# Layer 0's query projection as three products of split float32 values

## Chip, cores and metric

One core of one Trainium2 chip. The metric is the device time of one execution in microseconds (us); the kernel before has a median of 1353.7 us in 3 runs (1352.72 to 1354.24).

## What is computed

Two layers on x of shape (8, 512, 256), each a cross attention (16 heads of 16) and a feed-forward part. The change touches only layer 0's query projection:

```python
qp = (q @ Wq_w.T + Wq_b)          # q = layernorm(x), per batch (512, 256) @ (256, 256)
kp = (k @ Wk_w.T + Wk_b)          # k = ctx
vp = (v @ Wv_w.T + Wv_b)          # v = ctx
scores = einsum('bqhd,bkhd->bhqk', qp, kp) / sqrt(16)
```

The result `qp` is cut into three bfloat16 parts whose sum is the float32 value; attention multiplies those parts.

## The kernel before

`project_phase` is the first of three phases and takes the first 168 us. It runs over 8 batches, written out by hand, and in each makes, from the transposed context `CT`, layer 0's keys (k0), layer 0's values (v0), layer 1's keys (k1) and layer 1's values (v1), and from the normalised and transposed x, layer 0's queries (q0). It stores keys, queries and values to HBM, from where `attention_phase` loads them. Between phases all engines meet at the end of the block.

**TensorE** (L258 to L356), in each batch and in this order: k0 (`columns`, L291), two halves of v0 (`values`, L305), k1, the first half of v1, the transposes of normalised x into two PSUM banks (L338 to L342), the second half of v1 (L343), a count of masked keys (L345), and q0 (L350). `columns` makes two output tiles of 128x512 (m = 0, 1), each as a sum of two float32 products (c = 0, 1). In the profile each float32 matmul stands as two records, so q0's four matmuls are eight records. Seven PSUM banks go round; `room` waits until a bank's last reader is done.

**The copy of x** between the transposes and q0: ScalarE copies chunk 0 from PSUM to `XT` (L421) and VectorE copies chunk 1 (L565), each once per batch, in parallel. TensorE waits for both (L348, L349). `XT` has two buffers.

**ScalarE** (L407 to L425), per batch: `take` k0 (rest and first bfloat16 part, four copies), the square root of the normalisation, the second part of the last batch's q0, the second part of k0 (L401), `take` k1 (L394, four copies), the copy of x, the second part of k1, `take` q0 (L392). In batch 7 it issues nine DMAs of the next phase (`first_group`, L418) ahead of `take` k1.

**VectorE** (L547 to L578), per batch: v0 out of PSUM (L505), `normalize` (L492, L497), the third part of the last q0 (L523), the first half of v1 out, the copy of x (L565), the second half of v1 out, the next mask (L466), the next moments (L483), q0's remainder (`rest_of`, L516), the mask's sums. After batch 7 it runs a short tail (L580 to L592) whose L588 releases TensorE's L352, the last product before the phase ends.

**GpSimd** (L437 to L456) makes a few constants, then runs `split` for k0 and k1 of each batch: L433 subtracts the first part from the rest, L435 the second. ScalarE's second part (L401) waits for L433.

**SyncE** issues the loads and stores in program order. The query weight `wq0` is the 12th load (L217); its semaphore is `q_landed`.

Of the kernel before, what the change touches and what calls it, by code (L numbers as in the profile page):

```python
# [8 lines left out]
F32 = mybir.dt.float32  # L9
# [62 lines left out]
def project_phase(nc, dram, scratch, w, const):  # L72
# [3 lines left out]
    with ExitStack() as mem:  # L76
# [3 lines left out]
        def two(name, shape, dt):  # L80
            return [sb(f"{name}{i}", shape, dt) for i in range(2)]
# [10 lines left out]
        Z_sum = two("a_masked_sum", [P, T], BF16)  # L92
        X = two("a_x", [P, TT, D], F32)
        XN = two("a_xn", [P, TT, D], F32)
        XT = two("a_xT", [P, DC, T], F32)
        stats = two("a_stats", [P, TT, 6], F32)
        mv = two("a_mv", [P, TT, 2], F32)
        rstd = two("a_rstd", [P, TT], F32)
# [159 lines left out]
        @block.tensor  # L258
        def _(pe):
            def column_room(b, n, m):  # L260
                if n in by_pool:
                    pe.wait_ge(rounded[n], taken(n, b, m))
                else:
                    pe.wait_ge(remains[n], rest_made(n, b, m))

            def room(b, p):

                b, p = (b, p - 7) if p >= 7 else (b - 1, p + 5)
                if b < 0:
                    return  # L270
                if p in (0, 1):
                    column_room(b, "k0", p)
                elif p in (2, 3):
                    pe.wait_ge(v_out[0], 2 * b + p - 1)
                elif p in (4, 5):
                    column_room(b, "k1", p - 4)
                elif p in (6, 9):
                    pe.wait_ge(v_out[1], 2 * b + (1 if p == 6 else 2))
                elif p == 7:
                    pe.wait_ge(x_by_act, b + 1)  # L280
                elif p == 8:
                    pe.wait_ge(x_by_dve, b + 1)
                else:
                    column_room(b, "q0", p - 10)

            def out(b, p):
                return bank[(12 * b + p) % 7]

            first = {"k0": 0, "k1": 4, "q0": 10}

            def columns(b, n, src):  # L291

                for m in range(DC):
                    room(b, first[n] + m)
                    o = out(b, first[n] + m)
                    for c in range(DC):
                        mm = pe.matmul(o[:, :], w["w" + n][:, c, m * P:(m + 1) * P], src[:, c, :], start=(c == 0), stop=(c == DC - 1))  # L297
                    mm.then_inc(made[n], 1)

            def count(b):  # L300
                pe.wait_ge(mask_made, mask_summed(b))
                pe.matmul(count_bank[0:NB, :], pick[:, NB - 1 - b:2 * NB - 1 - b], Z_sum[b % 2][:, :], start=(b == 0),
                          stop=(b == NB - 1), skip_group_check=True).then_inc(counted, 1)

            def values(b, l, u):  # L305

                p = (2 + u) if l == 0 else (6, 9)[u]
                room(b, p)
                o = out(b, p)
                for j in range(2):  # L310
                    t = 2 * u + j
                    for c in range(DC):
                        mm = pe.matmul(o[:, j * D:(j + 1) * D], CT[b % 2][:, c, t * P:(t + 1) * P], w[f"wv{l}"][:, c, :], start=(c == 0), stop=(c == DC - 1))  # L313
                mm.then_inc(v_made[l], 1)

            pe.wait_ge(built, 7)
            for _ in range(8):
                pe.matmul(out(0, 11)[:, :], const["less"][:, 0:P], const["less"][:, :], start=True, stop=True)
            for b in range(NB):
                half = b % 2  # L320
                pe.wait_ge(ctx_landed[half], 16 * (b // 2 + 1))
                if b == 0:
                    pe.wait_ge(k0_landed, 32)
                columns(b, "k0", CT[half])
                if b == 0:
                    pe.wait_ge(v0_landed, 16)
                values(b, 0, 0)
                values(b, 0, 1)
                if b == 0:
                    pe.wait_ge(k1_landed, 16)  # L330
                columns(b, "k1", CT[half])
                if b == 0:
                    pe.wait_ge(one_landed, 48)
                values(b, 1, 0)
                if b == 0:
                    pe.wait_ge(cut, 3)
                pe.wait_ge(ln_out, (TT + 1) * (b + 1))
                for c in range(DC):  # L338
                    room(b, 7 + c)
                    for t in range(TT):  # L340
                        mm = pe.transpose(out(b, 7 + c)[:, t * P:(t + 1) * P], XN[half][:, t, c * P:(c + 1) * P], const["ident_f"][:, :])
                    mm.then_inc(x_turned, 1)  # L342
                values(b, 1, 1)  # L343
                for a in ([], [0, 1])[b] if b < 2 else [b]:
                    count(a)  # L345
                if b == 0:
                    pe.wait_ge(q_landed, 32)
                pe.wait_ge(x_by_act, b + 1)  # L348
                pe.wait_ge(x_by_dve, b + 1)  # L349
                columns(b, "q0", XT[half])  # L350
            pe.wait_ge(tail, 6)
            pe.matmul(count_bank[0:1, 0:1], left_top[:, :], const["ones"][0:NB, 0:1], start=True, stop=True).then_inc(counted, 1)  # L352
            keep_busy(pe, const, out(NB - 1, 7), 8)
            pe.wait_ge(tail, 7)
            const["flag"] = pe.value_load(const["general"][0:1, 0:1])
            keep_busy(pe, const, out(NB - 1, 7), 8)  # L356
# [5 lines left out]
        def _(act):  # L362
# [44 lines left out]
            for b in range(NB):  # L407
                half = b % 2
                if b == 0:
                    act.wait_ge(k0_landed, 32)  # L410
                take(b, "k0")
                act.wait_ge(ln_moments, 2 * TT * (b + 1))
                nc.scalar.activation(rstd[half][:, :], mv[half][:, :, 1], ACT.Sqrt, bias=const["eps"][:, 0:1], scale=16.0).then_inc(ln_std, 1)
                if b > 0:
                    next_part(b - 1, "q0")
                next_part(b, "k0")
                if b == NB - 1:
                    first_group()  # L418
                take(b, "k1")
                act.wait_ge(x_turned, 2 * b + 1)  # L420
                nc.scalar.activation(XT[half][:, 0, :], bank[(12 * b + 7) % 7][:, :], ACT.Copy).then_inc(x_by_act, 1)  # L421
                next_part(b, "k1")
                take(b, "q0")
            next_part(NB - 1, "q0")
# [3 lines left out]
        def _(pool):  # L428
# [21 lines left out]
            pool.wait_ge(cut, 8)  # L450
            nc.gpsimd.tensor_copy(qk0[:, :], qk[:, :]).then_inc(cut, 1)
            pool.wait_ge(cut, 9)
            nc.gpsimd.memset(qk0[0:1, 0:1], 0.0)
            for b in range(NB):
                split(b, "k0")
                split(b, "k1")  # L456
# [2 lines left out]
        def _(dve):  # L459
# [87 lines left out]
            for b in range(NB):  # L547
                if b == 0:
                    dve.wait_ge(bv0_landed, 32)
                values(b, 0, 0)  # L550
                values(b, 0, 1)
                normalize(b)
                if b == 0:
                    dve.wait_ge(q_landed, 32)
                    nc.vector.tensor_scalar(w["bq0"][:, :], w["bq0"][:, :], 0.25, None, ALU.mult).then_inc(small_made, 1)
                    dve.wait_ge(small_made, 1)
                    dve.wait_ge(one_landed, 48)
                if b > 0:
                    third_of(b - 1, "q0")
                if b == 1:  # L560
                    mask_of(1)
                    sum_mask(1)
                values(b, 1, 0)
                dve.wait_ge(x_turned, 2 * b + 2)
                nc.vector.tensor_copy(XT[b % 2][:, 1, :], bank[(12 * b + 8) % 7][:, :]).then_inc(x_by_dve, 1)  # L565
                values(b, 1, 1)
                if b == 0:
                    moments(1)
                    rest_of(0, "q0")
                    mask_of(0)  # L570
                    sum_mask(0)
                elif b + 1 < NB:
                    mask_of(b + 1)
                    moments(b + 1)
                    rest_of(b, "q0")
                    sum_mask(b + 1)
                if b == 1:
                    later_weights()  # L578
# [1427 lines left out]
def build(nc, dram):  # L2006

    with ExitStack() as ctx:
# [45 lines left out]
        with ExitStack() as first:  # L2054
            def wsb(name, shape, dt):
                return first.enter_context(nc.sbuf_tensor(name, shape, dt))

            early = {n: wsb(n, [P, DC, D], F32) for n in ("wk0", "wv0", "wq0", "wk1", "wv1")}
            early |= {n: wsb(n, [P, DC], F32) for n in ("bk0", "bq0")}
            early |= {n: wsb(n, [P, 2, D], F32) for n in ("bv0", "bv1")}  # L2060
            project_phase(nc, dram, scratch, w | early, const)
# [44 lines left out]
```

## Time and profile before

| | us |
|---|---|
| median of 3 runs | 1353.7 |
| lowest, highest | 1352.72, 1354.24 |
| the profiled execution's own time | 1358.95 |
| its span | 1357.2 |
| projection phase | 0 to 168 |
| TensorE busy in the span | 1259.6 (93%) |
| VectorE, ScalarE, GpSimd busy | 1003.9 (74%), 867.4 (64%), 511.7 (38%) |

The busy time of TensorE counts overlapping records once; a float32 128x512 record lasts 0.59 us while the next one starts 0.43 us after it, so the distance between starts is the price of a matmul and not its duration. The granted clock is 1.0 for 2.4 GHz and 0.5 for 1.2 GHz.

### The profile page before, as it was taken

The numbers are of one execution on the slowest core, as the hardware profiler recorded it, in microseconds if no ns is written. First come the engines' busy times: TensorE is split into PE (matmuls) and PEld (weight loads), VectorE is DVE, ScalarE is ACT, GpSimd is POOL, SyncE is SP. The second block draws the span as 40 slices with busy tenths as digits, with TensorE's granted clock in tenths as the row PEclk, the third lists the DMA queues.
The fourth block names the chain that finished last, engine by engine and source line by source line (L and its number), as shares of the span: only waits on it lengthen the run. The fifth ranks groups of instructions, "written<-read, shape, count | busy, mean of one in ns | idle before, by whom it ended". The sixth has DMA issues, their size and how long they took to land. (4 is left out here: it accounts for less than half of the span.)

```text
span 1357.2 us, 21436 instructions
## 1 busy us (share of the span) xinstructions
PE 1259.6 (93%) x7571; PEld 652.3 (48%) x7571; DVE 1003.9 (74%) x1724; ACT 867.4 (64%) x1483; POOL 511.7 (38%) x674
## 2 busy tenths in 40 slices
PE   8999989999999999999999999999998999980499
PEld 4565522334343343434455445545553785430298
DVE  5776788797878788786666688888773564996764
ACT  4455427676767777677665655665554666868693
POOL 3555400144353444435565433333333101656600
PEclk9999969999999999999999999999999999995699
DMA  7999774323334242333424553343201001326233
GB/s 242 379 328 329 284 180 115 104 64 93 96 113 127 63 136 79 111 99 100 118 78 115 153 173 95 104 120 98 63 18 48 1 0 47 140 93 232 78 109 109
DMA packets 88074, 170.82 MB, mean 126 GB/s; under 512 B 14742, under 2 KB 49310, under 8 KB 86430
## 3 DMA queue, kind: packets, MB, share of 16 engines
q1 hardware_dynamic: 87083, 167.37, 39.4%
q10 hardware_dynamic: 883, 2.05, 0.7%
q8 instruction: 63, 1.03, 0.3%
q14 instruction: 45, 0.37, 0.1%
HBM read 108.26 MB, written 60.31 MB: 124 GB/s over the span
## 5 line engine op out<-in xcount | busy, mean ns | idle before, releaser
L1342 DVE TENSOR_REDUCE b_neg_max<-b_score 128x1 f32<-128x512 f32 (+3 forms) x864 | 540.8, 662 | 177.8 <-PE b_score L887 93.6
L1112 ACT ACTIVATE b_probs<-b_exp 128x512 f32<-128x512 f32 (+1 forms) x864 | 463.2, 581 | 281.6 <-PE b_exp L911 280.7
L884 PE MATMUL b_score<-b_k_stack,b_q_stack 97*128 97x512 bf16 (+3 forms) x1024 | 355.9, 351 | 10.8 <-issue 4.9
L911 PE MATMUL b_exp<-b_q_stack,b_k_stack 100*128 100x512 bf16 (+3 forms) x1024 | 344.3, 341 | 6.4 <-ACT b_probs L1112 5.6
L932 PE MATMUL b_av<-b_probs,b_values 128*17 128x512 f32 (+3 forms) x2048 | 228.6, 518 | 3.7 <-POOL b_probs L1210 3.5
L884 PEld LDWEIGHTS b_score<-b_k_stack,b_q_stack 97*128 97x128 bf16 x1024 | 99.8, 98 | 246.8 <-DVE b_neg_max L1342 128.5
L911 PEld LDWEIGHTS b_exp<-b_q_stack,b_k_stack 100*128 100x128 bf16 x1024 | 100.1, 98 | 82.5 <-ACT b_probs L1112 24.8
L1210 POOL TENSOR_SCALAR_AFFINE_SELECT b_probs<-b_probs 128x512 f32<-128x512 f32 x96 | 61.7, 643 | 176.8 <-ACT b_probs L1112 176.3
L1218 POOL CAST b_max_parts<-b_neg_max 128x16 bf16<-128x16 f32 x64 | 12.9, 202 | 280.5 <-DVE b_neg_max L1342 278.2
L887 PE MATMUL b_score<-diag_qk,minus_big 128*128 128x128 bf16 x512 | 112.6, 220 | 0.0
L1626 PE MATMUL f_bank<-normed,f_w_upT 128*128 128x512 f32 x192 | 82.7, 592 | 0.0
L1810 POOL TENSOR_TENSOR f_hidden<-f_tmp,f_hidden 128x2048 int32<-128x2048 int32 x8 | 44.2, 5530 | 89.7 <-DVE f_tmp L1760 89.7
L932 PEld LDWEIGHTS b_av<-b_probs,b_values 128*17 128x17 f32 x2048 | 34.1, 95 | 76.5 <-issue 37.0
L968 PE MATMUL b_work<-wo,b_attendedT 128*128 128x256 f32 x256 | 61.5, 383 | 0.3 <-DVE b_x L1283 0.2
L433 POOL TENSOR_TENSOR a_rest_k<-a_rest_k,a_part_k 128x1024 f32<-128x1024 f32 x16 | 38.8, 2427 | 60.8 <-ACT a_part_k L392 49.4
L313 PE MATMUL a_bank<-wv,a_ctxT 128*128 128x256 f32 x256 | 60.5, 385 | 0.0
L887 PEld LDWEIGHTS b_score<-diag_qk,minus_big 128*128 128x128 bf16 x512 | 50.3, 98 | 20.4 <-issue 2.0
L297 PE MATMUL a_bank<-a_ctxT,wk 128*128 128x512 f32 x128 | 57.6, 593 | 0.8 <-DMA bk<-L_bk_in 0.8
L1626 PEld LDWEIGHTS f_bank<-normed,f_w_upT 128*128 128x128 f32 x192 | 36.4, 190 | 45.1 <-issue 43.0
L313 PEld LDWEIGHTS a_bank<-wv,a_ctxT 128*128 128x128 f32 x256 | 48.8, 193 | 13.3 <-issue 7.7
L61 PE MATMUL f_over<-less,ident_b 128*128 128x512 bf16 x31 | 9.7, 477 | 45.8 <-DVE f_hidden L1863 45.1
L968 PEld LDWEIGHTS b_work<-wo,b_attendedT 128*128 128x128 f32 x256 | 47.1, 189 | 9.8 <-DVE b_x L1283 2.1
(231 smaller groups left out, 2026.2 us busy)
## 6 DMA issues: line engine op xcount, KB each, us to landing
b_q_stack<-s_q SPq DMA_DIRECT2D x378, 64.0 KB
s_k<-a_part_k SPq DMA_DIRECT2D x48, 256.0 KB, 3.2
b_k_stack<-s_k SPq DMA_DIRECT2D x60, 192.0 KB
s_up<-f_up SPq DMA_DIRECT2D x6, 1536.0 KB, 5.1
s_va<-a_va SPq DMA_DIRECT2D x16, 544.0 KB, 5.4
b_values<-s_va SPq DMA_DIRECT2D x16, 544.0 KB, 4.2
a_mask_q<-mask_in SPq DMA_DIRECT2D x8, 1024.0 KB, 8.0
b_k_stack<-s_k SPq DMA_DIRECT2D x60, 128.0 KB
```

Source lines behind the costliest of these rows:

```text
L297: mm = pe.matmul(o[:, :], w["w" + n][:, c, m * P:(m + 1) * P], src[:, c, :], start=(c == 0), stop=(c == DC - 1))
L313: mm = pe.matmul(o[:, j * D:(j + 1) * D], CT[b % 2][:, c, t * P:(t + 1) * P], w[f"wv{l}"][:, c, :], start=(c == 0), stop=(c == DC - 1))
L884: mm = pe.matmul(o, q, KS[half][0:R_MAX, h, 0:w], start=True, stop=causal or not general)
L887: mm = pe.matmul(o[:, w - P:w], const["minus_big"][:, :], d[:, :], start=False, stop=True, skip_group_check=True)
L911: mm = pe.matmul(o, k, QS[half][0:NSTACK, h, q0:T], start=True, stop=not masked)
L932: mm = pe.matmul(av_bank[32 * j:32 * j + VW, q0:T], VA[n % 2][:, kc, 4 * g + j, :], probs[kc][:, j, q0:T], start=(kc == 0), stop=(kc == TT ...
L968: mm = pe.matmul(work[:, x * D:(x + 1) * D], src[:, c, y * P:(y + 1) * P], wt[:, c, :], start=(c == 0), stop=(c == DC - 1))
L1112: nc.scalar.activation(probs[kc][:, h0:h0 + m, q0:T], exp_bank[n % RINGS][:, 0:m * w].rearrange("p (h n) -> p h n", h=m), ACT.Exp).then_in ...
L1210: nc.gpsimd.affine_select(out=block, in_=block, fill=0.0, compare_op=ALU.is_ge, base=-1, pattern=[[0, 4], [1, P]], channel_multiplier=-1). ...
L1342: nc.vector.tensor_reduce(neg_max[u][:, qt, h0:h0 + m], score_bank[n % RINGS][:, 0:m * w].rearrange("p (h n) -> p h n", h=m), AX.X, ALU.ma ...
L1626: mm = pe.matmul(bank[f][:, :], w_upT[:, c, f * P:(f + 1) * P], xT[:, b, c, :], start=(c == 0), stop=(c == DC - 1))
L1810: nc.gpsimd.tensor_tensor(whole(b)[:, MINE:FC, :], sig[b % 2][:, MINE:FC, :], whole(b)[:, MINE:FC, :], ALU.mult).then_inc(act_by_pool, 1)
```

## The change

The float32 type "float32r" is a float32 word that TensorE multiplies at reduced precision. The change splits both operands of q0 into a float32r high value and the float32r remainder and sums three products of them: low weight times high x, high weight times high x, high weight times low x, for both c, so six matmuls per output tile and twelve per batch in place of four. The weights are split once on GpSimd, ahead of its first `split`; `query_low` lies on the bytes of `wq0`. x is split from PSUM in each batch: ScalarE copies both chunks to `XT_high`, VectorE subtracts both to `XT_low`, each chunk after ScalarE's copy of it. `XT_high` and `XT_low` have one buffer each. The other projections stay float32.

```diff
-        XT = two("a_xT", [P, DC, T], F32)
+        XT_high, XT_low = sb("a_xT_high", [P, DC, T], F32R), sb("a_xT_low", [P, DC, T], F32R)
+        query_high = sb("a_wq0_high", [P, DC, D], F32R)
+        query_low = nc.alloc_sbuf_tensor_at("a_wq0_low", [P, DC, D], F32R, offset=const["wq0_at"])
...
-                elif p == 7:
-                    pe.wait_ge(x_by_act, b + 1)
-                elif p == 8:
-                    pe.wait_ge(x_by_dve, b + 1)
+                elif p in (7, 8):
+                    pe.wait_ge(x_by_dve, DC * b + p - 6)
...
+            def queries(b):
+
+                for m in range(DC):
+                    room(b, first["q0"] + m)
+                    o = out(b, first["q0"] + m)
+                    terms = [(wt, src, c) for wt, src in ((query_low, XT_high), (query_high, XT_high), (query_high, XT_low)) for c in range(DC)]
+                    for k, (wt, src, c) in enumerate(terms):
+                        mm = pe.matmul(o[:, :], wt[:, c, m * P:(m + 1) * P], src[:, c, :], start=(k == 0), stop=(k == len(terms) - 1))
+                    mm.then_inc(made["q0"], 1)
...
                 if b == 0:
-                    pe.wait_ge(q_landed, 32)
-                pe.wait_ge(x_by_act, b + 1)
-                pe.wait_ge(x_by_dve, b + 1)
-                columns(b, "q0", XT[half])
+                    pe.wait_ge(cut, 12)
+                pe.wait_ge(x_by_dve, DC * (b + 1))
+                queries(b)
...
-                act.wait_ge(x_turned, 2 * b + 1)
-                nc.scalar.activation(XT[half][:, 0, :], bank[(12 * b + 7) % 7][:, :], ACT.Copy).then_inc(x_by_act, 1)
+                for c in range(DC):
+                    act.wait_ge(x_turned, DC * b + c + 1)
+                    nc.scalar.activation(XT_high[:, c, :], bank[(12 * b + 7 + c) % 7][:, :], ACT.Copy).then_inc(x_by_act, 1)
...
-            nc.gpsimd.memset(qk0[0:1, 0:1], 0.0)
+            nc.gpsimd.memset(qk0[0:1, 0:1], 0.0).then_inc(cut, 1)
+            pool.wait_ge(cut, 10)
+            pool.wait_ge(q_landed, 32)
+            nc.gpsimd.tensor_copy(query_high[:, :, :], w["wq0"][:, :, :]).then_inc(cut, 1)
+            pool.wait_ge(cut, 11)
+            nc.gpsimd.tensor_tensor(query_low[:, :, :], w["wq0"][:, :, :], query_high[:, :, :].bitcast(F32), ALU.subtract).then_inc(cut, 1)
...
-                dve.wait_ge(x_turned, 2 * b + 2)
-                nc.vector.tensor_copy(XT[b % 2][:, 1, :], bank[(12 * b + 8) % 7][:, :]).then_inc(x_by_dve, 1)
+                for c in range(DC):
+                    dve.wait_ge(x_by_act, DC * b + c + 1)
+                    nc.vector.tensor_tensor(XT_low[:, c, :], bank[(12 * b + 7 + c) % 7][:, :], XT_high[:, c, :].bitcast(F32), ALU.subtract).then_inc(x_by_dve, 1)
...
-            early = {n: wsb(n, [P, DC, D], F32) for n in ("wk0", "wv0", "wq0", "wk1", "wv1")}
+            const["wq0_at"] = nc.sbuf_base
+            early = {n: wsb(n, [P, DC, D], F32) for n in ("wq0", "wk0", "wv0", "wk1", "wv1")}
```

## Rows read from the trace of the kernel before

**Rows 1.** Busy time by stretch; then granted clock, DMA share and GB/s.

```profile
40.00:60.00 20.00, 17.68 (x59) 10.45 (x58) 15.01 (x29) 7.95 (x13) 8.49 (x4) 0.91 1.03 369
80.00:100.00 20.00, 20.00 (x72) 12.51 (x72) 14.53 (x29) 10.98 (x18) 10.47 (x5) 1.00 0.94 342
```

**Rows 2.** Timeline of TensorE, start and duration first: q0 of batches 3 and 6.

```profile
84.97 3.70 PE L297 MATMUL a_bank<-a_xT,wq 128*128 128x512 f32 x8
88.51 3.60 PE L297 MATMUL a_bank<-a_ctxT,wk 128*128 128x512 f32 x8
...
140.74 3.70 PE L297 MATMUL a_bank<-a_xT,wq 128*128 128x512 f32 x8
```

**Rows 3.** Timeline of TensorE: the gate product, 36 matmuls between these starts.

```profile
1059.89 0.71 PE L1637 MATMUL f_bank<-f_x_low,f_w_gate_high 128*128 128x512 f32 x2
...
1068.41 1.03 PE L1621 MATMUL f_turnx<-ident_f,f_tmp 128*128 128x128 f32 x8
```

**Rows 4.** Timeline of batch 3, from the transposes to q0.

```profile
81.60 2.72 POOL L433 TENSOR_TENSOR a_rest_k<-a_rest_k,a_part_k 128x1024 f32<-128x1024 f32 x1 [1.28 <-ACT a_part_k L394]
...
82.60 0.60 ACT L421 ACTIVATE a_xT<-a_bank 128x512 f32<-128x512 f32 x1 [1.08 <-PE a_bank L341]
...
83.04 0.69 DVE L565 COPY a_xT<-a_bank 128x512 f32<-128x512 f32 x1
...
84.36 1.06 ACT L401 ACTIVATE a_part_k<-a_rest_k 128x1024 bf16<-128x1024 f32 x1 [1.16 <-POOL a_rest_k L433]
...
84.66 0.38 PE L302 MATMUL a_counts<-a_masked_sum,a_pick 128*8 128x512 bf16 x1
84.84 0.69 DVE L505 TENSOR_TENSOR a_va<-a_bank,bv 128x512 f32<-128x512 f32 x1 [1.11 <-PE a_bank L313]
```

**Rows 5.** Groups by line and form: VectorE, two inputs, one from PSUM.

```profile
L1740 DVE TENSOR_TENSOR f_x_low<-f_turnx,f_x_high 128x512 fp32r<-128x512 f32 x8 | 5.5, 682 | 1.6 <-ACT f_x_high L1674 1.6
```

**Rows 6.** One line of VectorE, nearest kind: duration min/median/max in ns.

```profile
L516 DVE SCALAR_TENSOR_TENSOR a_rest_q<-a_bank,bq,a_part_q x16: 717/749/752, 27.8 to 164.3; 128x512 f32<-128x512 f32 x16
```

**Rows 7.** Groups by line and form: GpSimd's split of the gate weights.

```profile
L1454 POOL TENSOR_TENSOR f_w_gate_low<-f_w_gateT,f_w_gate_high 128x1536 fp32r<-128x1536 f32 x1 | 3.4, 3440 | 0.1
...
L1452 POOL CAST f_w_gate_high<-f_w_gateT 128x1536 fp32r<-128x1536 f32 x1 | 1.5, 1464 | 0.0
```

**Rows 8.** Issue of `wq0`'s load on SyncE's queue, and the tile's landing.

```profile
8.86 0.59 SPq L165 DMA_DIRECT2D wq<-L_wq_in  x1
...
DMA to landing us min/median/max: 6.5/6.5/6.5
```

**Rows 9.** Timeline of batch 0, GpSimd, VectorE, ScalarE and TensorE.

```profile
12.01 2.12 POOL L433 TENSOR_TENSOR a_rest_k<-a_rest_k,a_part_k 128x1024 f32<-128x1024 f32 x1 [7.86 <-ACT a_part_k L392]
...
15.54 5.11 DVE L497 TENSOR_SCALAR a_xn<-a_x,a_mv,a_rstd 128x256 f32<-128x256 f32 x4
...
17.25 0.59 ACT L394 ACTIVATE a_part_k<-a_bank 128x512 bf16<-128x512 f32 x1
...
20.75 1.06 PE L341 MATMUL a_bank<-ident_f,a_xn 128*128 128x128 f32 x8 [2.30 <-issue]
...
21.42 0.60 ACT L421 ACTIVATE a_xT<-a_bank 128x512 f32<-128x512 f32 x1 [3.57 <-PE a_bank L341]
...
24.69 3.97 PE L297 MATMUL a_bank<-a_xT,wq 128*128 128x512 f32 x8
```

**Rows 10.** Timeline of batch 1, VectorE and TensorE.

```profile
45.55 0.68 DVE L565 COPY a_xT<-a_bank 128x512 f32<-128x512 f32 x1
...
46.33 5.16 PE L297 MATMUL a_bank<-a_xT,wq 128*128 128x512 f32 x8 [0.87 <-issue]
```

**Rows 11.** Busy time by stretch, columns as in rows 1: batch 1's q0.

```profile
46.00:49.00 3.00, 2.67 (x3) 1.17 (x4) 2.32 (x4) 0.00 (x0) 1.31 (x1) 0.50 1.03 387
```

**Rows 12.** Timeline of batch 7, ScalarE and TensorE.

```profile
158.03 0.63 ACT L421 ACTIVATE a_xT<-a_bank 128x512 f32<-128x512 f32 x1
...
163.74 0.16 PE L352 MATMUL a_counts<-ones,a_left_top 8*1 8x1 bf16 x1 [0.70 <-DVE a_left_top L588]
```

## The prediction

> **What bounds the kernel now.** I read the busy time by stretch first. From 80 to 100 us TensorE is busy in 20.00 of 20 us at the full clock, VectorE in 14.53, ScalarE in 10.98, GpSimd in 10.47; the DMA engines move 342 GB/s at a share of 0.94, while the stretch from 40 to 60 reaches 369 [rows 1]. So TensorE sets the pace of the projection phase, with DMA close behind. The timeline of TensorE confirms it: q0 of batch 3 starts at 84.97, that of batch 6 at 140.74, three periods of 18.59 us to the hundredth, which is what an engine does that waits for nobody [rows 2]. Batches 2 to 6 look like that. Batches 0, 1 and 7 do not: TensorE idles before the transposes of batch 0 and before q0 of batch 1 [rows 9, 10], and after batch 7 it waits for VectorE's tail [rows 12]. The attention and feed-forward phases run the same instructions as before, so what the phase gains is kept, shifted.
>
> **The product itself.** In a steady batch q0 takes 88.51 - 84.97 = 3.54 us [rows 2]. A float32r matmul of the same shape is in this kernel already, in the gate product: 36 of them with their transitions take 1068.41 - 1059.89 = 8.52 us, 0.2367 each [rows 3]. Twelve are 2.84 us, so a batch saves 0.70 us of TensorE.
> The Trainium skill's page "FP8 and Floating Point Precision", section "TensorE Precision Notes", says that true float32 makes four passes and reduced float32 reads the word and truncates it. Counting passes alone, 16 would become 12, a quarter of q0, an estimate of 0.88 us per batch; the rows on the gate product give less, and the measurement decides.
>
> **The way to q0, steady batches.** Before, ScalarE copies chunk 0 at 82.60 and VectorE chunk 1 at 83.04, done at 83.73 [rows 4]. After, the chain is longer. ScalarE's first copy ends at 83.20; VectorE subtracts chunk 0 from about 83.25. ScalarE's second copy starts once the second transpose is in, about 83.1, and ends at 83.7. The subtraction of two 128x512 operands, one from PSUM, lasts 0.68 [rows 5]. The second one therefore ends at 83.25 + 2 x 0.68 = 84.61 at the latest. TensorE asks for it after the second half of v1 and the count, whose start is 84.66; q0 starts at 84.97 [rows 2, 4]. So the new chain ends nearly 0.4 us before its deadline, and costs nothing. If that cover is gone, each tenth past it is a tenth per batch.
> Who is behind it? On ScalarE the added 0.5 to 0.6 us falls in the 1.16 us in which L401 waits for GpSimd; on VectorE the added 0.7 falls in the 1.11 us in which L505 waits for TensorE [rows 4]. Both waits shrink, nothing is late. The single buffer of x costs nothing: ScalarE writes it only after the next transposes, which TensorE issues after the q0 that reads it. The same order covers the changed bank waits. SyncE issues nothing new; the DMAs only come closer together, 342 GB/s times 18.59 / 17.89 = 355, under the 369 seen [rows 1]. Five steady batches, 2 to 6: 5 x 0.70 = 3.5 us.
>
> **Does GpSimd block the subtraction?** Its L433 runs from 81.60 to 84.32 in just these microseconds [rows 4]. Sixteen VectorE operations of nearly the same kind, PSUM plus SBUF in, last 717 to 752 ns, never more, though some lie beside GpSimd's [rows 6]; the four normalisations of batch 0, which read SBUF only, take 5.11 us beside GpSimd's work [rows 9]. So I take no blocking.
>
> **Batch 0.** GpSimd now stands at the head of its queue waiting for `wq0`, with `split` of k0 behind it. The load is issued at 8.86 and lands 6.5 later, at 15.4 [rows 8]. The rows for the gate weights, three times as wide, give the two new operations: 1.46 / 3 = 0.49 and 3.44 / 3 = 1.15 us [rows 7]. L433, which ran at 12.01 for 2.12 [rows 9], now starts at about 17.1 and ends near 19.5, with some tenths for normalisations in between. ScalarE waits behind it: L401 (1.06) to 20.5, four copies of k1 at 0.5 each to 22.6, the two copies of x to 23.6; VectorE's second subtraction ends near 24.6. Before, q0 began at 24.69 [rows 9]. So the 3.57 us in which ScalarE waited for the transposes [rows 9] hide the whole shift, just. What is late next is the clock. VectorE's normalisations may be blocked less, the transposes come earlier than 20.75, and TensorE then idles ahead of q0 for up to 3.7 us. Before, q0 lasted 5.16 us in batch 1 after an idle stretch, at a granted clock of 0.50, the 1.2 GHz level, from 46 to 49 [rows 10, 11]. If the clock falls within q0 of batch 0, twelve matmuls at 1.2 GHz cost 0.43 each, +2.3 us. Bounds for the batch: a gain of 0.7 and a loss of 1.6. I take 0.
> The Trainium skill, page "SBUF — State Buffer", section "SBUF: two separate sides", calls the pair shared by VectorE and GpSimd an exclusive lock that the loser waits out. By it the order of GpSimd's operations, not their length, decides when the normalisations end; no number above uses that.
>
> **Batch 1.** VectorE is late here: the copy starts at 45.55, q0 at 46.33 [rows 10]. A second subtraction puts q0 at 46.9, 0.6 later. But the stretch at 1.2 GHz ends at a little over 49 all the same, so less of the work falls into it: from 46.9 to 49.3 some 5.6 matmuls at 0.43, then 6.4 at 0.237 = 1.5, done at 50.8 where it was 51.3 (5.0 us after 46.33). Bounds 0.1 and 1.2; I take 0.4.
>
> **Batch 7.** ScalarE is late by its nine DMA issues: its copy starts at 158.03, ends 158.66 [rows 12]. The second copy ends at 159.15, the subtractions at 159.4 and 160.0. q0 stood at 140.74 + 18.59 = 159.33 [rows 2], so it starts 0.7 later and ends where it ended: gain 0. VectorE's tail moves back 0.7 too, and TensorE already waits for it at 163.74 [rows 12]. The phase's end also hangs on the landing of the last keys, which doesn't move. Bounds 0 and 0.7 lost; I take 0.3.
>
> **Sum.** 3.5 + 0 + 0.4 + 0 - 0.3 = 3.6 us. The durations come from one profiled execution of 1358.95 us (span 1357.2), 5 us above the median; the saving should carry over: 1358.95 to 1355.35, the median 1353.7 to 1350.1. A measurement of this kernel can tell about 0.2%, 2.7 us, from no change.
>
> **Rivals.**
> A, the forecast, above: 1350.1, own range 1348.9 to 1352.0. Chance 0.60.
> B, a late handover in every batch. Semaphore steps from ScalarE to VectorE to TensorE longer than assumed, or GpSimd's L433 blocking the first subtraction until 84.32 after all, put the second one's end at 84.32 + 0.3 + 0.68 = 85.3 and q0 0.3 late in each steady batch. For: the overlap in time and the slack of only 0.4. Against: rows 6. Gain 3.6 - 5 x 0.3 = 2.1, 1351.6. Chance 0.15.
> C, DMA takes over. If the 342 GB/s of the steady stretch were its limit, the period could not shrink and the stalls would show as VectorE waiting for masks and x: only the 0.1 left of the ends, 1353.6. Against: 369 GB/s from 40 to 60 [rows 1]. Chance 0.13.
> D, slower, by GpSimd's wait in batch 0. The place is the wait for `q_landed` ahead of `split` of k0; every microsecond of it past 15.4 moves L433, L401, the copies of x and q0. The whole gain is gone if `wq0` lands at 19.0, 3.6 later. If it lands at 20.6, when VectorE's scaling of the bias first proves it there (the end of the 5.11 us that begin at 15.54 [rows 9]), and the clock falls within q0, it costs 5.2 + 2.3 against 3.6: 1357.6. For: the DMA engines are full at the start and that landing is one sample of a load whose place in the queue stays. Against: 6.5 us is this very tile's row [rows 8]. Chance 0.12, of it 0.04 between no change and 0.2%.
> That the change doesn't do what it says is hardly possible: the same form of product stands in the trace [rows 3].
>
> **How the numbers follow.** A gives faster by over 0.2% in most of its range, 0.50 of 0.60; B adds 0.05 of its 0.15: faster 0.55. C, the rest of A and B and 0.04 of D are no change: 0.37. Slower is 0.08. The range leaves out the slow part of D and little at the fast end: 1348.7 to 1353.7, which takes in B and C.
>
> **What would show it.** In the profile after: q0 as 12 records per batch in `queries`, nearly 0.24 us apart, 2.84 us in batches 2 to 6, and a period of 17.89 us (18.2 under B, 18.6 under C). No idle of TensorE ahead of q0 in those batches, a VectorE subtraction of 0.68 ending 0.4 ahead of it. GpSimd's first `split` at 17 and q0 of batch 0 near 24.7; the start of attention 3.6 us earlier. Wrong would be: a period above 18.0, L433 of batch 0 after 18, or an attention phase whose length changes by over 1 us.

## The result, and the profile after

The changed kernel takes 1359.10 us (median of 8 runs, 1356.56 to 1364.39) where the kernel before, on the same chip, takes 1354.19 (8 runs, 1352.72 to 1357.35): a ratio of 1.0039 with a 95% interval from 1.0028 to 1.0050. It is slower by 4 to 7 us, where 3.6 us less was forecast. A second measurement (below) gives 1357.52, 3.3 above the kernel before.

The profiled execution has a span of 1358.9 us. First the busy time by stretch, the same two stretches and columns as in [rows 1]:

```profile
40.00:60.00 20.00, 17.12 (x69) 11.73 (x68) 16.97 (x32) 9.88 (x16) 9.02 (x4) 1.00 1.02 367
80.00:100.00 20.00, 20.00 (x81) 13.93 (x80) 15.68 (x31) 11.58 (x19) 10.92 (x6) 1.00 0.97 346
```

The steady stretch is what the forecast had: TensorE without a gap, more matmuls in it, VectorE with 1.15 us more work per 20, DMA from 342 to 346 GB/s. Batch 3 in the timeline, which answers to [rows 2, 4]; start and duration first, in brackets the idle time before:

```profile
66.85 0.73 PE L307 MATMUL a_bank<-a_xT_high,a_wq_low 128*128 128x512 f32 x2
...
82.43 1.09 ACT L431 ACTIVATE a_xT_high<-a_bank 128x512 fp32r<-128x512 f32 x2 [1.08 <-PE a_bank L351]
83.06 1.29 DVE L581 TENSOR_TENSOR a_xT_low<-a_bank,a_xT_high 128x512 fp32r<-128x512 f32 x2 [0.30 <-ACT a_xT_high L431]
84.17 1.06 ACT L410 ACTIVATE a_part_k<-a_rest_k 128x1024 bf16<-128x1024 f32 x1 [0.66 <-POOL a_rest_k L443]
84.49 0.38 PE L312 MATMUL a_counts<-a_masked_sum,a_pick 128*8 128x512 bf16 x1
84.66 0.69 DVE L520 TENSOR_TENSOR a_va<-a_bank,bv 128x512 f32<-128x512 f32 x1 [0.32 <-PE a_bank L323]
84.80 0.74 PE L307 MATMUL a_bank<-a_xT_high,a_wq_low 128*128 128x512 f32 x2
...
87.69 2.74 PE L297 MATMUL a_bank<-a_ctxT,wk 128*128 128x512 f32 x6
```

q0 lasts 87.69 - 84.80 = 2.89 us, the period is 84.80 - 66.85 = 17.95. VectorE's second subtraction ends at 84.35, 0.45 us before TensorE's q0; the waits in which the added work was to fall are down from 1.16 to 0.66 on ScalarE and from 1.11 to 0.32 on VectorE. All of that is the forecast. Batch 0, which answers to [rows 7 to 9], isn't:

```profile
14.94 1.38 DVE L512 TENSOR_SCALAR a_xn<-a_x,a_mv,a_rstd 128x256 f32<-128x256 f32 x4
...
16.01 0.79 POOL L466 CAST a_wq_high<-wq 128x512 fp32r<-128x512 f32 x1 [11.87 <-DMA wq<-L_wq_in]
...
16.88 1.27 POOL L468 TENSOR_TENSOR a_wq_low<-wq,a_wq_high 128x512 fp32r<-128x512 f32 x1
...
18.10 2.14 POOL L443 TENSOR_TENSOR a_rest_k<-a_rest_k,a_part_k 128x1024 f32<-128x1024 f32 x1
...
18.41 1.04 PE L351 MATMUL a_bank<-ident_f,a_xn 128*128 128x128 f32 x8
...
20.27 1.06 ACT L410 ACTIVATE a_part_k<-a_rest_k 128x1024 bf16<-128x1024 f32 x1 [6.30 <-POOL a_rest_k L443]
...
23.14 1.11 ACT L431 ACTIVATE a_xT_high<-a_bank 128x512 fp32r<-128x512 f32 x2
...
23.80 1.29 DVE L581 TENSOR_TENSOR a_xT_low<-a_bank,a_xT_high 128x512 fp32r<-128x512 f32 x2 [4.40 <-ACT a_xT_high L431]
...
25.19 1.19 PE L307 MATMUL a_bank<-a_xT_high,a_wq_low 128*128 128x512 f32 x2 [4.02 <-issue]
...
26.18 1.05 PE L307 MATMUL a_bank<-a_xT_high,a_wq_high 128*128 128x512 f32 x2
...
30.44 1.10 PE L297 MATMUL a_bank<-a_ctxT,wk 128*128 128x512 f32 x2
```

The transposed x is ready in PSUM from 19.45, but ScalarE, waiting 6.30 us for GpSimd and then busy with k1, copies it at 23.14. TensorE idles 4.02 us, and a pair of matmuls then lasts 1.05 us where the steady batch has 0.62: q0 takes 30.44 - 25.19 = 5.25 us. Last, the start of the attention phase, in TensorE's timeline:

```profile
169.98 0.91 PE L900 MATMUL b_score<-b_k_stack,b_q_stack 97*128 97x512 bf16 x3 [4.37 <-issue]
171.14 0.61 PE L900 MATMUL b_score<-b_k_stack,b_q_stack 97*128 97x512 bf16 x1 [0.25 <-DVE b_neg_max L1358]
174.40 8.58 PE L900 MATMUL b_score<-b_k_stack,b_q_stack 97*128 97x512 bf16 x15 [2.65 <-issue]
```

Attention starts at 169.98, 2.74 us before the 172.72 of the first profile of before. But behind the fourth score matmul TensorE stops for 2.65 us, and "issue" says that no wait of the program is behind it. The kernel before has no such stop there.

### The profile page after: what moved, and what is told of

Read it like the earlier page. It is cut to its first block and busy times, and to the rows that moved or that the text cites. A ratio compares the mean times of both kernels' runs of the same rounds, so it can differ in the third digit from the quotient of the medians.

```text
span 1358.9 us, 21514 instructions
## 1 busy us (share of the span) xinstructions
PE 1255.3 (92%) x7599; PEld 659.0 (48%) x7603; DVE 1004.7 (74%) x1732; ACT 871.1 (64%) x1491; POOL 512.6 (38%) x676
## 5 line engine op out<-in xcount | busy, mean ns | idle before, releaser
L443 POOL TENSOR_TENSOR a_rest_k<-a_rest_k,a_part_k 128x1024 f32<-128x1024 f32 x16 | 38.7, 2421 | 46.1 <-ACT a_part_k L401 34.9
```

## The experiments

Each kernel was run 10 to 12 times beside the kernel before on the same chip; ratios are to that. "First score" is the start of TensorE's first score matmul, "to turn_max" the time from there to the first product that turns the row maxima (`b_exp<-ident_b,b_max_parts`): with its stop the changed kernel has 13.6 us, the first profile of before 11.5.

### Both kernels again

> The kernel before once more, unchanged, for a second profile: its one profile was of an execution of 1358.95 us, 5 us over the median. Theory P (the loss is made in the projection phase, in batches 0 and 1): a typical execution has the same projection phase as the profile, attention starting at 172.7, and its missing 5 us are elsewhere. Theory S (the loss is made behind the projection phase, by where the stretches at 1.2 GHz fall and how the attention phase starts): a typical execution has a shorter stretch at 1.2 GHz at the start of attention or none in batch 0 or 1, so about 5 us less between 160 and 210. Ratio 1.000 either way.

Measured: 1354.22 us, ratio 0.9999 (0.9988 to 1.0010).

> The changed kernel once more, unchanged, for a second profile. P: q0 of batch 1 ends near 51.8 as in the first profile and attention starts near 170. S: the start of attention near 170 repeats, and the time from there to the end is longer than in the kernel before by 4 to 7 us, in stalls or stretches at 1.2 GHz that lie at other places from one profile to the next. Ratio 1.003 to 1.005 either way.

Measured: 1357.52 us, ratio 1.0023 (1.0013 to 1.0034).

The ratio of the changed kernel was expected at 1.003 to 1.005; this second one is lower than the first, 1.0039, and the intervals overlap. What matters are the profiles. The execution of before that the prediction rests on took 1358.95 us, this one 1354.08, and the difference stands in batch 0:

```profile
14.37 3.19 DVE L497 TENSOR_SCALAR a_xn<-a_x,a_mv,a_rstd 128x256 f32<-128x256 f32 x4
...
17.83 1.04 PE L341 MATMUL a_bank<-ident_f,a_xn 128*128 128x128 f32 x8
18.46 0.60 ACT L421 ACTIVATE a_xT<-a_bank 128x512 f32<-128x512 f32 x1 [1.08 <-PE a_bank L341]
...
21.21 3.67 PE L297 MATMUL a_bank<-a_xT,wq 128*128 128x512 f32 x8 [0.61 <-DVE a_xT L565]
24.71 3.60 PE L297 MATMUL a_bank<-a_ctxT,wk 128*128 128x512 f32 x8
```

The normalisations took 3.19 us, not 5.11; ScalarE got to x at 18.46, not 21.42; q0 ran at 21.21 and at full clock [rows 9 for the other]. Batch 1 began at 24.71, not 28.50. So of the 5 us between that profile and the median, 3.8 lay in the very batch whose slack the forecast counted on. Neither theory had this: attention starts at 168.92, not at 172.7 (P), and from there to the last matmul the two executions differ by 1.1 us only (S). In the second profile of the changed kernel batch 1 begins at 30.10, the stop is there again (2.83 us), first score at 169.81, to turn_max 14.0 (r1_before_again: 11.3).

### GpSimd splits the query weights later

```diff
-            pool.wait_ge(cut, 10)
-            pool.wait_ge(q_landed, 32)
-            nc.gpsimd.tensor_copy(query_high[:, :, :], w["wq0"][:, :, :]).then_inc(cut, 1)
...
             for b in range(NB):
                 split(b, "k0")
+                if b == 0:
+                    pool.wait_ge(cut, 10)
+                    pool.wait_ge(q_landed, 32)
+                    nc.gpsimd.tensor_copy(query_high[:, :, :], w["wq0"][:, :, :]).then_inc(cut, 1)
...
                 split(b, "k1")
```

> GpSimd splits the query weights behind its two operations for k0 of batch 0, in place of ahead of them; all else as in the changed kernel. P: the wait for the load of the weights at the head of GpSimd's queue is what costs; q0 of batch 0 then starts at about 21.2 in place of 25.2, at 2.4 GHz, and ends 24.1 in place of 30.4; the kernel gains 4 to 6 us against the changed one: 1353 to 1355, ratio 0.999 to 1.001. S: the same gain up to the start of attention, but what attention does with it is open: anything from none of it to all, 1353 to 1359.

Measured: 1355.92 us, ratio 1.0012 (0.9999 to 1.0025). In its profile q0 of batch 0 starts at 21.06 at full clock, batch 1 at 23.93, and attention at 164.75, 4.2 us before r1_before_again. Then the stop takes 2.79 us, to turn_max 13.7. Theory P had 1353 to 1355. Two things follow: the wait at the head of GpSimd's queue costs batch 0 some microseconds, and something after the projections takes all of them back: the span is 1354.1 us, that of r1_before_again 1352.3.

### The clock held through batches 0 and 1

```diff
+                if b < 2:
+                    room(b, 10)
+                    keep_busy(pe, const, out(b, 10), (18, 9)[b])
                 pe.wait_ge(x_by_dve, DC * (b + 1))
```

> The changed kernel with 18 filler matmuls (128x512, bf16, about 0.21 us each) ahead of q0 in batch 0 and 9 in batch 1, so that TensorE does not idle there; they write to q0's own bank, which q0 overwrites. P: q0 in batch 0 stays at 2.4 GHz, 2.9 us in place of 5.2, in batch 1 likewise; gain 2 us against the changed kernel, 1357. S: the same in the projection phase; the total moves by anything between -4 and +4.

Measured: 1355.62 us, ratio 1.0011 (1.0001 to 1.0022). The granted clock stays at 1.00 to the end of the projections, but batch 1 still begins at 29.91 and first score stays at 169.89: the fillers run until 26.94, 3.6 us after x is split (23.34), and the first two products of batch 0, k0 and v0, took 9.18 us in this execution where r1_before_again has 6.96. What else differs is that the stop is gone.

```profile
169.89 10.94 PE L903 MATMUL b_score<-b_k_stack,b_q_stack 97*128 97x512 bf16 x19 [4.53 <-issue]
```

Nineteen in a row, as before. What differs ahead of this point is TensorE's instruction stream: the change makes it 32 matmuls longer, this kernel 27 more. (Matmuls are counted here as the profile's records: q0 has 12 for 8 in each of 8 batches.) That was the new theory: the stop hangs on the place in the stream.

### The kernel before with a longer stream

```diff
-            for _ in range(8):
-                pe.matmul(out(0, 11)[:, :], const["less"][:, 0:P], const["less"][:, :], start=True, stop=True)
+            for _ in range(40):
+                pe.matmul(out(0, 11)[:, 0:102], const["less"][:, 0:P], const["less"][:, 0:102], start=True, stop=True)
```

> The kernel before, with its 8 warm-up matmuls of 512 columns replaced by 40 of 102 columns: the same columns, 32 matmuls more in TensorE's instruction stream, as many as the change adds by the time the attention begins. Theory 1 (the stop of 2.65 to 2.83 us behind the fourth score matmul, put down to issue, hangs on the position in TensorE's instruction stream): the first score matmuls stand as x4 and x15 with 2.7 us between, first score to first turn_max 13.7 us instead of 11.3, and the time is 1356.5 us, 2.5 above before. Theory 2 (the stop comes of the split product or of the shifted times of the loads): x19 in a row, 11.3 us, 1354.1 us.

Measured: 1357.14 us, ratio 1.0021 (1.0011 to 1.0031).

```profile
167.30 1.44 PE L884 MATMUL b_score<-b_k_stack,b_q_stack 97*128 97x512 bf16 x3 [4.53 <-issue]
171.56 9.15 PE L884 MATMUL b_score<-b_k_stack,b_q_stack 97*128 97x512 bf16 x16 [2.83 <-issue]
```

The kernel before, with no part of the change in it, gets the stop of 2.83 us (behind three or four matmuls; some records are missing), 14.0 us to turn_max, and 3.0 us more in the median. This is the run that decides: the stop comes of the number of instructions ahead of it, not of the split product. The 3.0 us are not all the stop's: the 1.2 GHz stretch at the start of attention lasts 31 us in this profile, 24 in r1_before_again.

> r5_before_longer with 28 matmuls of 16 columns more, 4 ahead of each query product of batches 1 to 7: the stream is 60 matmuls longer than in the kernel before, close to the 59 of r4_hold_clock. Theory 1 (position): the stop of 2.83 us is gone again, first score to first turn_max 11.4 us; the small matmuls cost 0.2 us a batch or so, 1.4 us in all, so the median is 1357.1 - 2.5 + 1.4 = 1356.0 us. Rival (any longer stream has the stop): first score to first turn_max 14.0 us and 1358.5 us.

```diff
+                if b > 0:
+                    room(b, 10)
+                    for _ in range(4):
+                        pe.matmul(out(b, 10)[:, 0:16], const["ident_b"][:, :], const["less"][:, 0:16], start=True, stop=True)
                 pe.wait_ge(x_by_act, b + 1)
```

(Added to the edit above.) Measured: 1356.05 us, ratio 1.0017 (1.0004 to 1.0031), with 19 score matmuls in a row from 169.52 and 11.5 us to turn_max. The period is 18.69 us where before had 18.59, so the small matmuls cost 0.6 us in six batches, less than the 1.4 expected; that the stop went is plain in the profile, the gain in the time is not separated from these costs.

### The changed kernel with a longer stream

```diff
-            for _ in range(8):
-                pe.matmul(out(0, 11)[:, :], const["less"][:, 0:P], const["less"][:, :], start=True, stop=True)
+            for _ in range(35):
+                pe.matmul(out(0, 11)[:, 0:117], const["less"][:, 0:P], const["less"][:, 0:117], start=True, stop=True)
```

> The changed kernel, unchanged but for 35 warm-up matmuls of 117 columns instead of 8 of 512: 27 matmuls more in TensorE's stream and nothing else, no filler that could hold the clock. Theory 1 (the stop of 2.7 us behind the fourth score matmul hangs on the position in the stream): x19 in a row, first score to first turn_max 11.4 us instead of 13.6 to 14.0, median 1357.5 - 2.5 = 1355.0 us; what is left against before, 1.0 us, is batch 0. Theory 2 (in r4_hold_clock it was the held clock of batches 0 and 1 that took the stop away): the stop stays, 1357.5 us.

Measured: 1354.78 us, ratio 1.0005 (0.9990 to 1.0021), against 1357.52 and 1359.10. Nothing else is changed and no filler holds a clock (it falls in batch 0, to a mean of 0.67 from 24 to 28 us). The first score starts at 168.16, 11.3 us to turn_max:

```profile
168.16 0.95 PE L900 MATMUL b_score<-b_k_stack,b_q_stack 97*128 97x512 bf16 x3 [4.36 <-issue]
169.32 9.57 PE L900 MATMUL b_score<-b_k_stack,b_q_stack 97*128 97x512 bf16 x16 [0.22 <-DVE b_neg_max L1358]
```

### The later split with a longer stream

The same edit on r3_split_later, with 35 matmuls of 117 columns (r6), 26 of 157 (r7) or 21 of 195 (r11); r7 has this too:

```diff
+                if b == 1:
+                    room(b, 10)
+                    keep_busy(pe, const, out(b, 10), 9)
                 pe.wait_ge(x_by_dve, DC * (b + 1))
```

> r3_split_later with 35 warm-up matmuls of 117 columns instead of 8 of 512: 27 matmuls more in the stream, as r4_hold_clock had. Theory 1 (position): x19 in a row, first score to first turn_max 11.4 us instead of 13.75, first score at 164.8; median 1355.92 - 2.4 = 1353.5 us. Theory 2 (the stop comes with the split product wherever the attention does not start late): the stop stays at 2.7 us and the median at 1355.9.

Measured: 1354.81 us, ratio 0.9996 (0.9983 to 1.0009), where 1353.5 was expected. The stop is gone, 11.5 us to turn_max. First score at 169.81, not 164.8: in this execution the normalisations of batch 0 took 4.51 us, and the clock was at 0.50 for parts of batch 1.

> r3_split_later with 26 warm-up matmuls of 157 columns and 9 fillers ahead of the query product of batch 1: the stream is 27 matmuls longer as in r6_split_later_longer, and the clock should hold through batch 1's query product. Theory 1: from the query product of batch 1 to that of batch 2 18.0 us instead of 19.5, first score at 163.4, no stop among the first scores, median 1352.2 us. Rival: the fillers only delay and the 1.5 us come back as a later start of batch 1's query product: 164.8 and 1353.5.

Measured: 1352.83 us, ratio 0.9985 (0.9972 to 0.9998). From q0 of batch 1 to that of batch 2 18.04 us, first score at 163.31, as theory 1 had it, and no stop. But only part of the 5.6 us by which attention starts sooner than in r1_before_again reaches the end (span 1350.9 against 1352.3). The busy time by stretch shows where most of the rest went; r1_before_again first, then r7_split_hold:

```profile
170.00:190.00 20.00, 19.25 (x39) 4.02 (x39) 19.37 (x34) 2.47 (x3) 1.36 (x7) 0.50 0.98 210
190.00:194.00 4.00, 4.00 (x15) 1.33 (x14) 3.23 (x5) 3.00 (x6) 0.32 (x2) 0.61 0.51 124
194.00:198.00 4.00, 4.00 (x27) 1.06 (x25) 3.29 (x6) 3.20 (x7) 0.00 (x0) 1.00 0.34 89
```

```profile
164.00:170.00 6.00, 6.00 (x11) 0.93 (x9) 6.00 (x11) 0.00 (x0) 0.00 (x0) 0.50 1.03 229
170.00:190.00 20.00, 18.94 (x44) 4.67 (x44) 17.59 (x30) 5.96 (x9) 1.67 (x8) 0.50 0.87 182
190.00:194.00 4.00, 4.00 (x15) 0.71 (x14) 1.72 (x3) 1.41 (x3) 0.00 (x0) 0.55 0.18 52
194.00:198.00 4.00, 4.00 (x25) 1.26 (x27) 3.49 (x7) 3.23 (x7) 0.00 (x0) 1.00 0.61 160
```

Attention begins at the 1.2 GHz level (0.50) in both, behind an idle stretch of TensorE of 4.6 to 4.7 us, and in both the full clock is back by 194, although one started 5.6 us sooner. Counted from the first turn_max, the third one comes 3.0 us later in r7_split_hold. The rest went near 1050, where its granted clock fell as well and that of r1_before_again did not.

> r3_split_later with 21 warm-up matmuls of 195 columns instead of 8 of 512: 13 matmuls more in the stream, so what stood behind the fourth score matmul stands 9 matmuls ahead of the first. Theory 1 (a point in the instruction stream at which TensorE waits for what comes next): no stop among the score matmuls, and either a longer stop ahead of them than 4.2 to 4.7 us (it adds up) or none (TensorE stops there anyway); with none the median is 1355.9 - 2.5 = 1353.4 us, with all of it 1355.9. Rival: the stop stays behind the fourth score matmul, 1355.9 us.

Measured: 1352.30 us, ratio 0.9985 (0.9971 to 0.9999). No stop behind any score matmul, 4.37 us ahead of them, as much as without it: theory 1 with "TensorE stops there anyway", though a stop that has moved ahead of them isn't seen as such. Its batch 0 was a poor one in this execution (normalisations 6.43 us, batch 1 at 28.28). This and r7_split_hold are the versions that beat both kernels, by 1.9 and 1.3 us at the medians; the intervals, 0.01% to 0.29% and 0.02% to 0.28%, just leave out no change. r6_split_later_longer is r11_split_later_13 but for 14 warm-up matmuls, has no stop either, and is 2.5 us slower; nothing here says why, so the 1.9 us of the best of the four versions with the later split say little about that version.

### The wait on its own, in the kernel before

```diff
...
+            pool.wait_ge(q_landed, 32)
+            nc.gpsimd.tensor_copy(query_high[:, :, :], w["wq0"][:, :, :]).then_inc(cut, 1)
+            pool.wait_ge(cut, 11)
+            nc.gpsimd.tensor_tensor(query_high[:, :, :], w["wq0"][:, :, :], query_high[:, :, :].bitcast(F32), ALU.subtract).then_inc(cut, 1)
             for b in range(NB):
```

> The kernel before, with GpSimd rounding and subtracting the query weights at the head of its queue as the changed kernel does, behind the wait for their load; the results are not read, and the query product stays as it was. Theory 1 (it is this wait that costs batch 0): copies of k1 held to 21.5 us, query product of batch 0 at 25.2 instead of 21.2 and at half clock (5.2 us for 3.5 us), first key product of batch 1 at 30.4, first score 4 us or more later than 168.9, median 1358 us. Rival (the loss in batch 0 comes of the split product's own longer chain of copies, six behind the transposes): query product at 21.2 to 22, median within 0.5 us of 1354.

Measured: 1355.68 us, ratio 1.0014 (1.0002 to 1.0027). The profile has the chain that was expected, here without any split product:

```profile
15.64 0.66 POOL L457 CAST a_wq_high<-wq 128x512 fp32r<-128x512 f32 x1 [11.50 <-DMA wq<-L_wq_in]
...
19.82 1.06 ACT L402 ACTIVATE a_part_k<-a_rest_k 128x1024 bf16<-128x1024 f32 x1 [5.69 <-POOL a_rest_k L434]
...
22.70 0.62 ACT L422 ACTIVATE a_xT<-a_bank 128x512 f32<-128x512 f32 x1
```

```profile
23.42 5.13 PE L298 MATMUL a_bank<-a_xT,wq 128*128 128x512 f32 x8 [2.65 <-ACT a_xT L422]
28.39 1.88 PE L298 MATMUL a_bank<-a_ctxT,wk 128*128 128x512 f32 x4
```

ScalarE waits for GpSimd, x is copied at 22.70, TensorE idles 2.65 us and q0 runs for 28.39 - 23.42 = 4.97 us instead of 3.5. The rival is out. It is 1.8 us from here to the 25.19 of the changed kernel: 0.4 by a load that came earlier, the rest by what the split puts behind the first copy of x (25.09 - 23.14 = 1.95 us against 0.62). The median rose by 1.5 us where 4 were expected; the 21.2 I had set it against is a good batch 0, which not every execution of before has, and this profile is of an execution of 1360.53 us, 4.9 above its own median.

## Why the prediction was wrong

**Where the time went.** I put the two second profiles side by side, r1_before_again and r2_after_again; their spans differ by 3.3 us, near the measured 1.0023. First key product of batch 1: 24.71 and 30.10, lost 5.4. From there to the first score: 168.92 - 24.71 = 144.21 and 169.81 - 30.10 = 139.71, gained 4.5. First score to the last matmul's start (1348.06 and 1351.30): 1179.14 and 1181.49, lost 2.35. Sum: 3.2 us slower.

**Step "The product itself": right.** 2.89 us for 2.84 forecast, period 17.95 for 17.89; a batch gains 0.64 for 0.70.

**Step "The way to q0" and rivals B and C: right, both out.** The slack was 0.45 us where nearly 0.4 was forecast, no idle ahead of q0 in batches 2 to 6. VectorE's subtraction beside GpSimd's L443 took 1.29 us for two, so nothing blocked it. DMA gave way.

**Steps "Batch 1" and "Batch 7": neither as reasoned.** The forecast had part of batch 1's q0 at 1.2 GHz. Batch 1 had no such stretch in the changed kernel: from its q0 to that of batch 2 17.95 us where before had 66.38 - 46.33 = 20.05. Against that its q0 came 18.46 us after the batch's beginning where it had been 17.83, so batch 1 gained 1.5, above the upper bound of 1.2. The sign came right, but not by the way reasoned, and the size is not the change's alone: over the profiles this q0 runs at 1.2 GHz, in whole or in part, in both kinds of kernel (before, r1, r8; r3, r6, r11) and at full clock in both (r5, r10; after, r2, r9). In batch 7 VectorE was late by 0.64 (0.7 forecast) and q0 made it up; from q0 of batch 2 to the first score the changed kernel gains 106.34 - 103.13 = 3.2 us, just the five steady batches, so batch 7 came to 0 and not to 0.3 lost.

**Step "Batch 0", "I take 0": wrong**, in two ways. In its own working it was short by little: the weights landed in time for GpSimd at 16.01, not 15.4, and each link of the chain followed (the two GpSimd operations 0.79 and 1.27 us for 0.49 and 1.15, L443 at 18.10 for 17.1, the second subtraction's end at 25.09 for 24.6). The fall of the clock, priced at 2.3 us and not taken, came. That is 28.50 to 30.44, 1.9 us lost, where the bound was 1.6. What it was set against was worse: the 24.69 of [rows 9] is one execution, in which the normalisations took 5.11 us and the clock had fallen too. Over the profiles batch 1 begins at 28.50, 24.71, 24.98 and 26.37 without the wait (before, r1, r5, r10; mean 26.1), and at 30.44, 30.10 and 28.77 with it (after, r2, r9; mean 29.8); r8, with the wait alone, has 28.39, and the later split, with the split product but no wait, 23.93, 26.33, 23.41 and 28.28 (r3, r6, r7, r11; mean 25.5). The changed kernel's mean lies 3.6 us behind that of before, with spreads of 1.7 and 3.8 in so few profiles, so this is known to some 2 us only. The loss lies in rival D's place, with a load that came nearly on time. The slack was not there to be used.

**"The attention and feed-forward phases run the same instructions as before, so what the phase gains is kept": wrong.** They run the same instructions at another place in the stream. Adding 32 matmuls to before costs 3.0 us by itself (r5_before_longer), and 27 more give the changed kernel 2.7 back (r9_after_longer), 1.1 in each of the other two such pairs (r3 to r6, r5 to r10, the latter with 0.6 of added matmuls). No rival had this. The sign of "what would make it wrong" was right: an attention phase whose length changes by over 1 us. First score to last matmul is 1180.24 in the first profile of before and 1184.64 after. Of these 4.4 us the stop brought 2.1 by the first turn_max. For the rest the clock differs: the 1.2 GHz stretch at attention's start lasts some 27 us, not 24, and the clock falls near 1020 too (granted 0.57 from 1020 to 1024). That longer stretch stands without the stop as well (r4, r8), so the stop isn't its only cause. A fall near 1050 comes and goes between executions, of before too; one near 1020 stands in three of the four profiles with the stop (after, r3, r5) and in none of the nine without it. Nothing here settles what decides them.

Without the stop the changed kernel is where before is (1.0005); with the weights' split moved behind k0's as well it is 0.04% (r6_split_later_longer) or 0.15% faster (r11_split_later_13). So the saved product exists in the profiles, 3.2 us in five steady batches, and the wait in batch 0 takes a good part of it, but in the time the wait is worth less than the 3.6 us of the profiles: by the ratios 1.2 to 2.7 us (r9 to r6 or r11, r2 to r3, before to r8), each known to about 2 us. With the 3 us of the stop that is 4 to 6 of the 7 to 8.5 us between forecast and measurement. What the remaining 1 to 4 us are is not shown; the stretches of lower clock are where the profiles differ.

## What to carry to other kernels

Read the stretch in which you count on slack from more than one execution, above all where the profiled one is not at the median: here 3.8 of its 5 us lay in the very batch whose slack was to hide the new wait. A wait put at the head of an engine's queue is priced by the whole chain behind it and by what TensorE's idle time does to the clock, not by its own length. When the number of instructions changes, look ahead of the first matmuls of the next phase for new idle time put down to "issue", and try a few matmuls more before judging the edit itself: here 13 to 28 cheap ones took 1.1 to 3.6 us off the median.

## What the hardware showed that was not expected

**A stop that hangs on the place in the instruction stream.** By matmuls ahead of attention, counted from before, with the product split or not: 0 none (before, r1, r8), 32 a stop of 2.65 to 2.83 us (after, r2, r3, r5), 45 none (r11), 59 or 60 none (r4, r6, r7, r9, r10). The DMA queues of the changed kernel from 168 to 176 us:

```profile
q1 hardware_dynamic: 325, 1.01, 56.6%
q10 hardware_dynamic: 257, 0.70, 36.8%
q8 instruction: 1, 0.02, 1.5%
```

One packet of instructions among 582 of data (columns: packets, MB, share of 16 engines), with the DMA engines otherwise full. But r1_before_again, which has no stop, shows the same in its 168 to 176 us:

```profile
q8 instruction: 1, 0.02, 1.2%
```

Read in steps of 1 us, every one of the thirteen profiles has such a packet 2 to 4 us before the first score and one within 4 us behind it; only the four with the stop have a further one 10 to 11 us behind it. So the packets fall at other places when the stop is there, but a packet beside the scores does not make a stop. That TensorE waits for its next instructions behind the loads of attention would fit, and the engine's 4.2 to 5.4 us of "issue" before every first score too; but the trace doesn't say whose packet it is, and no run took the loads away, so this cause is argued and not shown. That the number of matmuls ahead decides whether the stop is there is shown.

**Normalisations that last 1.38 to 6.43 us.** The same four VectorE operations of batch 0 take 1.38 us where GpSimd does nothing in their first 1.07 us or more: while it waits for the load (after, r2), or in a gap between its operations (r3, r5). Where it starts or works within their first 0.6 us they take 2.70 to 6.43 us (5.14 in r10, 6.43 in r11), and so they do behind the wait too: 4.53 in r9, where the load landed at 15.30. The rule of the Trainium skill's page "SBUF — State Buffer", section "SBUF: two separate sides", that the shared pair is an exclusive lock, agrees with these numbers. So in the first profile after, the wait on GpSimd even left the step ahead of the transposes undisturbed, and it bought nothing: the transposes stood at 18.41 and ScalarE came at 23.14.

**An early start does not end a slow stretch.** The full clock came back at 193 to 200.5 us in every profile, whether attention had begun at 163.3 or at 172.7; r7_split_hold spent some 31 us at 1.2 GHz, r1_before_again 24. So microseconds gained in the projections may be lost there again, and a change of 1 us ahead of that point can't be read from the time.
